# Mamba and expert block on one core: gate folded into the output weights, residual one sequence ahead, moments by aggregation, B two steps ahead, new slots

## The chip, the cores and the metric

The kernel runs on one core of a Trainium2 chip. A core has five engines with a queue of instructions each: TensorE (PE; its weight loads PEld), VectorE (DVE), ScalarE (ACT), GpSimd (POOL) and SyncE (SP), which here only issues DMAs. An engine works its own queue in order; between engines the order is kept by semaphores that an instruction raises and another waits for. Work goes on in SBUF (128 partitions) and PSUM (where TensorE writes). The metric is device microseconds for the whole program.

## The reference

For each of 16 sequences of 512 tokens with 128 features, all in f32:

```
h  = layernorm(x) * (1 + ca) + sa                        # sa, ca, ga, sb, cb, gb: rows per sequence
xn = layernorm(h) * norm_g + norm_b
for each direction d (forward, backward in time):
    u, z = split(xn @ Win.T);  u = silu(conv4(u) + convb)  # 256 channels
    dtr, B, C = split(u @ Wx.T);  dt = softplus(dtr @ Wdt.T + bdt)
    s_t = exp(dt_t * A) * s_(t-1) + (dt_t * u_t) * B_t     # 16 states per channel
    y_d = ((C_t . s_t) + u * D) * silu(z) @ Wout.T
x2  = x + ga * (h + y_f + y_b)
h2  = layernorm(x2) * (1 + cb) + sb
moe = shared swiglu(h2) + sum over the best 2 of 8 experts of weight * swiglu_e(h2)
out = x2 + gb * moe
```

## The kernel before

Everything is unrolled. `passes` calls `body(b, ...)` for b = 0 to 16. Pass b does the state scans of sequence b and, a sequence behind, the expert stage of sequence fb = b - 1; the preparation of sequence b + 1 (two normalizations, the forward direction's u, B, C, dt, z) runs in the same pass. A pass has 32 slots (`STEPS`): slot d*16 + n is the scan step of direction d and state n. Pass 0 has no expert stage, pass 16 has only that. Before pass 0 a prologue runs the preparation of sequence 0 alone.

Each engine's queue is written out by hand, slot by slot, from tables at the head (lines 30 to 38): `PREP_SLOT` and the `_AT` numbers say in which slot a step of a preparation stands, and `LN_SLOT`, `FX_SLOT`, `LN3_SLOT`, `H2T_SLOT`, `GATE_SLOT`, `UP_SLOTS`, `DOWN_SLOTS` do so for the rest. What stands in a slot per engine:

- GpSimd: `bmul` (L426) writes `bt` = v * B for the slot after (both halves, 128x1024), into one of two buffers; it waits until the scans of the slot two before the written one are done. Then `side`: `norms` (`moments`, eight small operations that turn the statistics into a reciprocal deviation and a shift; the scale and shift of h), `make_dt`, `make_v`. Then `ffn_side`: the residual `x2` (L511, L514), the moments of the third normalization, the router's weights, and `act` (L526), the product of the two up projections.
- VectorE: `scan` (L787), two halves in place in `psA`; `read_out` (L797), `g` = state * C, half 0; `expert_silu` (L882), `pf`; `read_out` half 1; then the side work: `statistics` (L803), `silu` (L823), the gate of y, `fx` (L907), the router (`gate`), `expert_sum` (L896) for each expert.
- ScalarE: `expert_turns` (L681 `tf`, L684 `gf`) from the up projections' banks; `exps` (L600), the decay exponentials of the next slot into `psA`, half by half, each after that half's read-out; `ln1p` (L648), whose `Ln` needs another function table than `Exp` and `Tanh`; the copy `h1K`; `normalize`; `silu`'s `Tanh` (L621) and the dt pieces. At slots 0 and 16 `keep_y` stands ahead of all.
- TensorE: `sum_y` (L987) of the slot before; `ffn_late` (projection L1085, turn of `zF` L1093, router L1098, half a down projection L1112 per slot); `prep` and the skip path; `expert_up` (L1068, L1071), one half of one expert per slot. There is one bank F0 and one F1, so each up projection waits for `pf` of the one before.
- SP: loads of B and C rows (`rows_in`) every other slot; at slot 0 the loads for the pass.

The gate `ga` multiplies `fx` = projection + h in `x2` = fx * ga + x, with x loaded a second time (`xR`). The functions that the change touches:

## Time and profile before

| what | value |
|---|---|
| timed runs | 2583.35, 2583.36, 2584.0 us (median 2583.36) |
| profiled execution, its own time | 2582.57 us |
| its span in the trace | 2580.8 us |
| granted TensorE clock, mean | 0.911 |
| HBM read, written | 285.91 MB, 6.34 MB |
| first scan starts, last scan ends | 87.0 us, 2495.0 us |

The span is the time between the first and the last instruction in the trace. Shares of busy time are averages over the prologue, 16 passes with scans and the tail. Times in a timeline are counted from the span's start; where a row merges several instructions its length is theirs together.

### The profile page before, as it was taken

How to read it: one execution, taken by the hardware profiler on the slowest of the kernel's cores; microseconds unless marked ns; L12 is line 12 of the kernel's file. 1: busy time of each engine (PE TensorE's matmuls, PEld its weight loads, DVE VectorE, ACT ScalarE, POOL GpSimd, SP SyncE). 2: the span in 40 equal slices, each digit the busy share in tenths (PEclk: the TensorE clock that was granted, in tenths of full speed). 3: DMA queues.
4: the chain of work that ended last, by engine and by line, in shares of the span. 5: the costliest groups of instructions: out<-in, count | busy, mean ns of one | idle time of the engine just before them, and what ended most of it. 6: DMA issues, size and time to landing. Idle time of an engine off the chain costs nothing. (4 is left out here: it accounts for less than half of the span.)

```text
span 2580.8 us, 31577 instructions
## 1 busy us (share of the span) xinstructions
PE 2100.5 (81%) x9893; PEld 1343.5 (52%) x9893; DVE 2284.9 (89%) x3603; ACT 1509.0 (58%) x2468; POOL 1957.8 (76%) x1437
## 2 busy tenths in 40 slices
PE   3677887978788897888879788897878879887868
PEld 1244554545555455555545555454555545555545
DVE  1699998999999899998989899899999989999973
ACT  2546656655566665656666555666556566555633
POOL 1577878778787877878877787877878787787854
PEclk8777998989899898998989899898989989899998
DMA  3334342333433333333333424333332433333310
GB/s 82 128 129 134 105 138 101 116 123 112 136 105 123 118 110 129 114 125 107 116 124 116 140 99 132 107 111 129 115 132 98 138 106 115 128 106 130 112 68 5
DMA packets 120557, 294.32 MB, mean 114 GB/s; under 512 B 18516, under 2 KB 53172, under 8 KB 120388
## 3 DMA queue, kind: packets, MB, share of 16 engines
q1 hardware_dynamic: 120388, 292.30, 33.7%
q8 instruction: 78, 1.28, 0.2%
q14 instruction: 91, 0.75, 0.1%
HBM read 285.91 MB, written 6.34 MB: 113 GB/s over the span
## 5 line engine op out<-in xcount | busy, mean ns | idle before, releaser
L426 POOL TENSOR_TENSOR bt<-v,bb 128x1024 f32<-128x1024 f32 x512 | 1208.4, 2363 | 158.7 <-DVE psA L787 154.6
L787 DVE TENSOR_TENSOR_SCAN psA<-psA,bt 128x512 f32<-128x512 f32 x1024 | 1197.3, 1215 | 100.7 <-POOL bt L426 81.1
L600 ACT ACTIVATE psA<-dt,aneg 128x512 f32<-128x512 f32 x1024 | 688.2, 688 | 813.0 <-DVE g L797 807.4
L987 PEld LDWEIGHTS psY<-ident,g 128*128 128x128 f32 x4096 | 515.4, 151 | 461.8 <-issue 241.6
L987 PE MATMUL psY<-ident,g 128*128 128x128 f32 x4096 | 605.5, 294 | 149.5 <-DVE g L797 149.4
L797 DVE TENSOR_TENSOR g<-psA,cb 128x512 f32<-128x512 f32 x1024 | 672.5, 676 | 0.0
L526 POOL TENSOR_TENSOR act<-pf,gf 128x512 f32<-128x512 f32 x288 | 366.8, 1273 | 248.4 <-DVE pf L882 216.2
L1068 PE MATMUL F<-h2T,w 128*128 128x512 f32 x576 | 333.9, 663 | 90.5 <-DVE pf L882 90.5
L1112 PE MATMUL F<-w,act 128*128 128x128 f32 x2304 | 319.8, 284 | 44.4 <-POOL act L526 41.1
L1112 PEld LDWEIGHTS F<-w,act 128*128 128x128 f32 x2304 | 292.2, 198 | 61.8 <-POOL act L526 55.3
L1071 PE MATMUL F<-h2T,w 128*128 128x512 f32 x576 | 307.5, 616 | 0.0
L882 DVE SCALAR_TENSOR_TENSOR pf<-tf,F 128x512 f32<-128x512 f32 x288 | 194.6, 676 | 64.4 <-ACT tf L681 62.7
L1003 PE MATMUL psP<-xnT,wcT 128*128 128x512 f32 x512 | 247.0, 606 | 5.2 <-DVE zs L823 2.2
L681 ACT ACTIVATE tf<-F 128x512 f32<-128x512 f32 x288 | 169.7, 589 | 63.7 <-PE F L1068 63.7
L684 ACT ACTIVATE gf<-F 128x512 f32<-128x512 f32 x288 | 172.4, 599 | 47.6 <-PE F L1071 47.5
L1068 PEld LDWEIGHTS F<-h2T,w 128*128 128x128 f32 x576 | 96.9, 200 | 197.4 <-DVE pf L882 139.0
L1071 PEld LDWEIGHTS F<-h2T,w 128*128 128x128 f32 x576 | 116.2, 202 | 150.9 <-issue 150.4
L1019 PE MATMUL psP<-xnT,wzT 128*128 128x512 f32 x128 | 99.2, 867 | 83.3 <-DVE zs L823 80.6
L896 DVE SCALAR_TENSOR_TENSOR facc<-F,wts,facc 128x128 f32<-128x128 f32 x512 | 143.0, 341 | 8.5 <-PE F L1112 8.5
L1003 PEld LDWEIGHTS psP<-xnT,wcT 128*128 128x128 f32 x512 | 89.6, 195 | 73.1 <-issue 64.8
L472 POOL TENSOR_TENSOR dt<-xb,ab 128x1024 f32<-128x1024 f32 x32 | 75.2, 2351 | 38.2 <-ACT ab L648 38.2
L1016 PE MATMUL psP<-xd,wdtT 8*128 8x512 f32 x128 | 91.2, 799 | 14.8 <-ACT xd L630 9.9
(133 smaller groups left out, 1709.1 us busy)
## 6 DMA issues: line engine op xcount, KB each, us to landing
bb<-bc_rows SPq DMA_DIRECT2D x256, 512.0 KB, 3.7
cb<-bc_rows SPq DMA_DIRECT2D x256, 512.0 KB, 3.6
x<-in_L_attn_x SPq DMA_DIRECT2D x16, 256.0 KB, 4.8
xR<-in_L_attn_x SPq DMA_DIRECT2D x16, 256.0 KB, 4.4
out_x<-osb SPq DMA_DIRECT2D x16, 256.0 KB, 4.8
w<-in_L_ffn_ew SPq DMA_DIRECT2D x2, 1024.0 KB
modA<-mod_table SPq DMA_DIRECT2D x16, 128.0 KB, 4.6
bc_rows<-xd SPq DMA_DIRECT2D x32, 64.0 KB, 3.2
```

The lines of the kernel that those rows point to most:

```text
L426: g.tensor_tensor(bt[:, n % 2, :, :], v[d][:, :, :], bb[:, n // 2 % 2, n % 2, :].unsqueeze(1).broadcast_to([P, NH, T]), ALU.mult).then_inc ...
L526: g.tensor_tensor(act[:, k // 2 % 3, k % 2, :], pf[:, k % 2, :], gf[:, k % 3, :], ALU.mult)\
L600: s.activation(psA[:, half * T:half * T + T], dt_[d][:, half, :], ACT.Exp, scale=aneg[d][:, half, n:n + 1]).then_inc(a_s, 1)
L684: s.activation(gf[:, k % 3, :], F1[:, :], ACT.Copy).then_inc(F1_free, 1)
L787: w.tensor_tensor_scan(ah, ah, bt[:, n % 2, half, :][:, order], 0.0, ALU.mult, ALU.add)\
L797: w.tensor_tensor(g_[:, n % 2, half, :], psA[:, half * T:half * T + T], cb[:, n // 2 % 2, n % 2, :], ALU.mult).then_inc(g_s, 1)
L882: w.scalar_tensor_tensor(pf[:, k % 2, :], tf[:, k % 2, :], 1.0, F0[:, :], ALU.add, ALU.mult).then_inc(pf_s, 1)
L987: last = m.matmul(psY[:, half * T + i * P:half * T + i * P + P], g_[:, n % 2, half, i * P:i * P + P], ident[:, :], is_transpose=True, star ...
L1003: last = m.matmul(psP[:, :], wcT[d][:, half, j, :], xnT[:, lo:lo + T], start=(j == 0), stop=(j == TAPS - 1))
L1068: m.matmul(F0[:, :], w1[:, x_, half * P:half * P + P], h2T[:, :], start=True, stop=True)\
L1071: m.matmul(F1[:, :], w2[:, x_, half * P:half * P + P], h2T[:, :], start=True, stop=True)\
L1112: last = m.matmul(F2[:, i * D:i * D + D], act[:, e % 3, half, i * P:i * P + P], w3[:, ORDER[e], half, :], start=(half == 0), stop=(half == 1))
```

## The change

- `ga` is multiplied into a copy of the output weights of both directions (`wg`), once per sequence on GpSimd at slot 25 (`gated_weights`), from a row `modG` that SP loads at slot 4. The projection uses `wg`.
- The residual hx = h * ga + x is made by GpSimd while sequence b + 1 is prepared (slots 21 and 23), and copied by ScalarE to `hxK`. `x2` is then one VectorE operation, projection + hxK. The second load of x and two GpSimd operations go; `load` of the next x waits for hx.
- `statistics` is followed by a memset and four aggregations (`bn_aggr`) on VectorE, after a wait for the statistics; `moments` has four operations instead of eight.
- `bmul` writes `bt` two slots ahead; it stands first in the slot, as before, and waits for the scan of its own slot.
- After `Ln` the table of `Exp` is loaded at once (`preload_act_table`). The Z pieces stand a slot later, `make_v` a slot earlier.
- The slots of the normalizations, of the third normalization, the router, the up and the down projections are new; the turn of `zF` moves from `ffn_late` to `expert_up`, behind the preparation in TensorE's queue.

The diff, cut to what is added and removed with the functions that it stands in:

```diff
-U_AT, XD_AT, DT_AT, LN1P_AT, Z_AT, V_AT = 0, 6, 7, 9, 9, 11
-LN_SLOT, XN_SLOT = 9, 16
+U_AT, XD_AT, DT_AT, LN1P_AT, Z_AT, V_AT = 0, 6, 7, 9, 10, 11
+STAT_SLOT, RSTD_SLOT, Z1_SLOT, H1_SLOT, STAT2_SLOT, RSTD2_SLOT, XNORM_SLOT, XN_SLOT = 8, 9, 10, 12, 13, 14, 15, 16
+HX_SLOT, WG_SLOT = 21, 25
-POSTB_SLOT, PROJ_SLOT, FX_SLOT, LN3_SLOT, H2T_SLOT, GATE_SLOT = 1, 3, 5, 6, 8, 9
-UP_SLOTS = [slot for slot in range(9, 28) if slot not in (22,)]
-DOWN_SLOTS = [slot for slot in range(12, 32) if slot not in (19, 21)]
+POSTB_SLOT, PROJ_SLOT, X2_SLOT, LN3_SLOT, H2T_SLOT, GATE_SLOT = 1, 3, 4, 4, 6, 7
+UP_SLOTS = [slot for slot in range(7, 28) if slot not in (9, 10, 22)]
+DOWN_SLOTS = [slot for slot in range(11, 32) if slot not in (13, 14, 25)]
...
             def load(b):
-                wait(sp, h1_s, 2 * b)
+                wait(sp, hx_s, 2 * b)
-                row = mod_dram[bass.ds(b, 1), 0:2 * D].broadcast_to([P, 2 * D])
+                row = mod_dram[bass.ds(b, 1), 0:3 * D].broadcast_to([P, 3 * D])
...
+                    if scan and slot == X2_SLOT:
+                        wait(sp, wg_s, b)
+                        row = mod_dram[bass.ds(b, 1), 2 * D:3 * D].broadcast_to([P, D])
+                        sp.dma_start(modG[:, :], row).then_inc(modG_in, 16)
...
-                    for k, kind in enumerate((2, 5)):
-                        row = mod_dram[bass.ds(fb, 1), kind * D:kind * D + D].broadcast_to([P, D])
-                        sp.dma_start(modF[:, k, :], row).then_inc(modF_in, 16)
+                    row = mod_dram[bass.ds(fb, 1), 5 * D:6 * D].broadcast_to([P, D])
+                    sp.dma_start(modF[:, :], row).then_inc(modF_in, 16)
-                    sp.dma_start(xR[:, :, :], t["x"][bass.ds(fb, 1)].rearrange("a (k p) d -> p (a k) d", p=P))\
-                        .then_inc(xR_in, 16)
...
-            def moments(st_, stat_, rstd_, sig, q):
-                g.tensor_tensor(stat_[:, :, 0:2], st_[:, :, 1:3], st_[:, :, 4:6], ALU.add).then_inc(sig, 1)
-                g.tensor_tensor(stat_[:, :, 2:3], st_[:, :, 1:2], st_[:, :, 4:5], ALU.subtract).then_inc(sig, 1)
+            def moments(stat_, rstd_, sig, q):
+                g.tensor_tensor(stat_[:, :, 2], stat_[:, :, 1], epsilon[:, :], ALU.add).then_inc(sig, 1)
+                g.tensor_tensor(stat_[:, :, 3], stat_[:, :, 0], negative[:, :], ALU.mult).then_inc(sig, 1)
-                g.tensor_tensor(stat_[:, :, 0:3], stat_[:, :, 0:3], scales[:, :, :], ALU.mult).then_inc(sig, 1)
+                g.tensor_tensor(rstd_[:, :], stat_[:, :, 2], mhalf[:, :], ALU.pow).then_inc(sig, 1)
-                g.tensor_tensor(stat_[:, :, 3:4], stat_[:, :, 2:3], stat_[:, :, 2:3], ALU.mult).then_inc(sig, 1)
-                pool.wait_ge(sig, q + 4)
-                g.tensor_tensor(stat_[:, :, 4:5], stat_[:, :, 1:2], stat_[:, :, 3:4], ALU.add).then_inc(sig, 1)
-                pool.wait_ge(sig, q + 5)
-                g.tensor_tensor(stat_[:, :, 5], stat_[:, :, 4], epsilon[:, :], ALU.add).then_inc(sig, 1)
-                pool.wait_ge(sig, q + 6)
-                g.tensor_tensor(rstd_[:, :], stat_[:, :, 5], mhalf[:, :], ALU.pow).then_inc(sig, 1)
-                pool.wait_ge(sig, q + 7)
-                g.tensor_tensor(stat_[:, :, 6], stat_[:, :, 0], rstd_[:, :], ALU.mult).then_inc(sig, 1)
+                g.tensor_tensor(stat_[:, :, 4], stat_[:, :, 3], rstd_[:, :], ALU.mult).then_inc(sig, 1)
             def norms(b, slot):
-                if slot == LN_SLOT + 1:
+                if slot == RSTD_SLOT:
-                    pool.wait_ge(lnA, 8 * b + 4)
+                    pool.wait_ge(lnA, 16 * b + 8)
-                    moments(st, stat, rstd, rstdA, 16 * b)
-                if slot == LN_SLOT + 3:
+                    moments(stat, rstd, rstdA, 8 * b)
+                if slot == H1_SLOT:
-                if slot == LN_SLOT + 5:
-                    pool.wait_ge(lnA, 8 * b + 8)
-                    moments(st, stat, rstd, rstdA, 16 * b + 8)
+                if slot == HX_SLOT:
+                    wait(pool, hxK_s, b)
+                    g.tensor_tensor(hx[:, :, :], z1[:, :, :], over_tiles(modA[:, 2, :]), ALU.mult).then_inc(hx_s, 1)
+                if slot == HX_SLOT + 2:
+                    pool.wait_ge(hx_s, 2 * b + 1)
+                    g.tensor_tensor(hx[:, :, :], hx[:, :, :], x[:, :, :], ALU.add).then_inc(hx_s, 1)
+                if slot == RSTD2_SLOT:
+                    pool.wait_ge(lnA, 16 * b + 16)
+                    moments(stat, rstd, rstdA, 8 * b + 4)
...
-                if slot == GATE_SLOT + 4:
+                if slot == GATE_SLOT + 6:
-                if slot == FX_SLOT:
-                    pool.wait_ge(F2_free, (DOWN + 1) * fb + PROJ + 1)
-                    pool.wait_ge(modF_in, 48 * fb + 48)
-                    wait(pool, o_s, 2 * fb)
-                    g.tensor_tensor(x2[:, :, :], fx[:, :, :], over_tiles(modF[:, 0, :]), ALU.mult).then_inc(x2_s, 1)
-                    pool.wait_ge(x2_s, 2 * fb + 1)
-                    pool.wait_ge(xR_in, 16 * fb + 16)
-                    g.tensor_tensor(x2[:, :, :], x2[:, :, :], xR[:, :, :], ALU.add).then_inc(x2_s, 1)
-                if slot == LN3_SLOT:
-                    pool.wait_ge(lnF, NT * fb + NT)
+                if slot == LN3_SLOT + 1:
+                    pool.wait_ge(lnF, 8 * fb + 8)
-                    moments(stF, statF, rstdF, rstdF_s, 8 * fb)
+                    moments(statF, rstdF, rstdF_s, 4 * fb)
...
+            def gated_weights(b):
+                pool.wait_ge(modG_in, 16 * b + 16)
+                wait(pool, F2_full, (DOWN + NE) * (b - 1) + PROJ + 1)
+                g.tensor_tensor(wg[:, :, :, :].rearrange("p a k d -> p (a k) d"),
+                                wout_both[:, :, :, :].rearrange("p a k d -> p (a k) d"),
+                                over_tiles(modG[:, :]), ALU.mult).then_inc(wg_s, 1)
             def side(b, slot, prep_b, prep_f, post_f):
+                if post_f and slot == WG_SLOT:
+                    gated_weights(b)
-                    if slot == PREP_SLOT[0] + V_AT:
+                    if slot == PREP_SLOT[0] + V_AT - 1:
-                if prep_b and slot == PREP_SLOT[1] + V_AT:
+                if prep_b and slot == PREP_SLOT[1] + V_AT - 1:
+            bmul(1, 0, 1)
                     if scan:
-                        nxt = slot + 1
+                        nxt = slot + 2
-                            bmul(STEPS * b + nxt, 0, 0)
+                            bmul(STEPS * b + nxt, 0, nxt - STEPS)
...
+                s.preload_act_table(ACT.Exp)
             def normalize(dst, x_, stat_, rstd_, sig):
-                                 bias=stat_[:, i, 6:7]).then_inc(sig, 1)
+                                 bias=stat_[:, i, 4:5]).then_inc(sig, 1)
             def norms(b, slot):
-                if slot == LN_SLOT + 2:
-                    act_e.wait_ge(rstdA, 16 * b + 8)
-                    wait(act_e, h1K_s, b)
+                if slot == Z1_SLOT:
+                    act_e.wait_ge(rstdA, 8 * b + 4)
+                    wait(act_e, hx_s, 2 * b)
-                if slot == LN_SLOT + 6:
-                    act_e.wait_ge(rstdA, 16 * b + 16)
+                if slot == XNORM_SLOT:
+                    act_e.wait_ge(rstdA, 8 * b + 8)
...
                     if scan:
-                        if slot == FX_SLOT + 2:
+                        if slot == X2_SLOT + 2:
-                            act_e.wait_ge(h1_s, 2 * b + 2)
-                            s.activation(h1K[:, :, :], z1[:, :, :], ACT.Copy).then_inc(h1K_s, 1)
+                            act_e.wait_ge(hx_s, 2 * b + 2)
+                            s.activation(hxK[:, :, :], hx[:, :, :], ACT.Copy).then_inc(hxK_s, 1)
...
-            def statistics(x_, st_, sig):
+            def statistics(x_, st_, stat_, sig, q):
+                dve.wait_ge(sig, q + NT)
+                w.memset(stat_[:, :, 4], 0.0)
+                for i in range(NT):
+                    w.bn_aggr(stat_[:, i, 0:2], st_[:, i, :]).then_inc(sig, 1)
             def norms(b, slot):
-                if slot == LN_SLOT:
+                if slot == STAT_SLOT:
-                    wait(dve, rstdA, 16 * b)
-                    statistics(x, st, lnA)
-                if slot == LN_SLOT + 4:
+                    wait(dve, rstdA, 8 * b)
+                    statistics(x, st, stat, lnA, 16 * b)
+                if slot == STAT2_SLOT:
-                    statistics(z1, st, lnA)
+                    statistics(z1, st, stat, lnA, 16 * b + 8)
...
             def ffn_side(fb, slot):
-                if slot == FX_SLOT:
+                if slot == X2_SLOT:
-                    dve.wait_ge(h1K_s, fb + 1)
+                    dve.wait_ge(hxK_s, fb + 1)
-                    w.tensor_tensor(fx[:, :, :], F2[:, :].rearrange("p (k c) -> p k c", c=D), h1K[:, :, :], ALU.add)\
+                    w.tensor_tensor(x2[:, :, :], F2[:, :].rearrange("p (k c) -> p k c", c=D), hxK[:, :, :], ALU.add)\
                 if slot == LN3_SLOT:
-                    dve.wait_ge(x2_s, 2 * fb + 2)
-                    wait(dve, rstdF_s, 8 * fb)
-                    statistics(x2, stF, lnF)
-                if slot == GATE_SLOT + 1:
+                    dve.wait_ge(F2_free, (DOWN + 1) * fb + PROJ + 1)
+                    wait(dve, rstdF_s, 4 * fb)
+                    statistics(x2, stF, statF, lnF, 8 * fb)
+                if slot == GATE_SLOT:
...
             def expert_up(fb, slot):
+                if slot == H2T_SLOT:
+                    pe.wait_ge(zF_s, NT * fb + NT)
+                    pe.wait_ge(F2_free, free + H2T)
+                    for i in range(NT):
+                        last = m.transpose(F2[:, i * P:i * P + P], zF[:, i, :], ident[:, :])
+                    last.then_inc(F2_full, 1)
...
+                        pe.wait_ge(wg_s, fb + 1)
-                                            woutT[k // NH][:, k % NH, :], start=(k == 0), stop=(k == 2 * NH - 1))
+                                            wg[:, k // NH, k % NH, :], start=(k == 0), stop=(k == 2 * NH - 1))
-                if slot == H2T_SLOT:
-                    pe.wait_ge(zF_s, NT * fb + NT)
-                    pe.wait_ge(F2_free, free + H2T)
-                    for i in range(NT):
-                        last = m.transpose(F2[:, i * P:i * P + P], zF[:, i, :], ident[:, :])
-                    last.then_inc(F2_full, 1)
```

## Rows read from the trace of the kernel before

**Rows 1.** Busy time of each engine, from the page.

```profile
PE 2100.5 (81%) x9893; PEld 1343.5 (52%) x9893; DVE 2284.9 (89%) x3603; ACT 1509.0 (58%) x2468; POOL 1957.8 (76%) x1437
```

**Rows 2.** Windows, all engines: start:end, length, busy (count), clock, DMA share, GB/s.

```profile
0.00:87.01 87.01, 34.75 (x73) 13.56 (x73) 11.63 (x47) 25.28 (x47) 15.49 (x35) 0.82 0.30 86
87.01:214.49 127.48, 86.81 (x330) 52.36 (x331) 119.62 (x147) 68.61 (x108) 92.43 (x55) 0.75 0.38 132
977.87:1130.53 152.66, 129.90 (x617) 83.12 (x616) 142.15 (x225) 93.58 (x154) 122.23 (x90) 0.91 0.36 119
```

**Rows 3.** Waits of VectorE in the pass at 977.87: total, times, longest.

```profile
DVE psA L787 <- POOL bt L426: 4.9, 5, 1.6
DVE pf L882 <- ACT tf L681: 1.9, 1, 1.9
DVE zs L823 <- ACT th L621: 1.6, 1, 1.6
DVE psA L787 <- ACT psA L600: 0.9, 4, 0.2
DVE acc L841 <- PE psP L1026: 0.5, 1, 0.5
DVE facc L896 <- PE F L1112: 0.4, 1, 0.4
```

**Rows 4.** Timeline, slot 4 and the start of ScalarE after it: start, length.

```profile
997.76 2.34 DVE L787 TENSOR_TENSOR_SCAN psA<-psA,bt 128x512 f32<-128x512 f32 x2 [0.23 <-ACT psA L600]
...
1000.02 1.27 DVE L797 TENSOR_TENSOR g<-psA,cb 128x512 f32<-128x512 f32 x2
...
1001.20 0.68 DVE L823 SCALAR_TENSOR_TENSOR u<-th,psP 128x512 f32<-128x512 f32 x1
...
1000.73 1.30 ACT L600 ACTIVATE psA<-dt,aneg 128x512 f32<-128x512 f32 x2 [0.78 <-DVE g L797]
```

**Rows 5.** VectorE: group MAX8; timeline of four, and of one set of statistics.

```profile
L853 DVE MAX8 top<-gl 128x8 f32<-128x8 f32 x64 | 5.8, 152 | 0.0
...
1027.62 0.36 DVE L853 MAX8 top<-gl 128x8 f32<-128x8 f32 x4
...
1005.83 0.86 DVE L803 BATCH_NORM_STATS2 stF<-x 128x6 f32<-128x128 f32 x4
```

**Rows 6.** Timeline of GpSimd, slots 5 to 7 of the same pass.

```profile
1002.56 1.27 POOL L511 TENSOR_TENSOR x<-fx,modF 128x512 f32<-128x512 f32 x1 [3.77 <-DVE fx L907]
...
1007.45 0.20 POOL L433 TENSOR_TENSOR statF<-stF 128x8 f32<-128x8 f32 x1
...
1010.13 0.20 POOL L447 TENSOR_TENSOR statF<-statF,rstdF 128x4 f32<-128x4 f32 x1
```

**Rows 7.** Groups of GpSimd, from the page: busy, mean ns, idle before.

```profile
L426 POOL TENSOR_TENSOR bt<-v,bb 128x1024 f32<-128x1024 f32 x512 | 1208.4, 2363 | 158.7 <-DVE psA L787 154.6
...
L526 POOL TENSOR_TENSOR act<-pf,gf 128x512 f32<-128x512 f32 x288 | 366.8, 1273 | 248.4 <-DVE pf L882 216.2
```

**Rows 8.** Timeline of ScalarE, slots 7 to 16 of the same pass.

```profile
1012.24 1.63 ACT L652 ACTIVATE zF<-x,statF,rstdF 128x128 f32<-128x128 f32 x4
...
1020.71 1.28 ACT L648 ACT_TABLE_LOAD   x1
...
1022.00 1.06 ACT L648 ACTIVATE ab<-ab 128x1024 f32<-128x1024 f32 x1
...
1055.80 1.08 ACT L608 ACTIVATE acc<-psY 128x512 f32<-128x512 f32 x2 [0.68 <-PE psY L987]
...
1056.77 0.60 ACT L681 ACTIVATE tf<-F 128x512 f32<-128x512 f32 x1
```

**Rows 9.** Timeline of ScalarE before the first scan.

```profile
76.63 0.60 ACT L621 ACTIVATE th<-psP 128x512 f32<-128x512 f32 x1 [1.65 <-PE psP L1019]
```

**Rows 10.** Timeline of VectorE and ScalarE in the tail.

```profile
2507.57 0.69 DVE L907 TENSOR_TENSOR fx<-F,h1K 128x512 f32<-128x512 f32 x1 [3.99 <-PE F L1085]
...
2514.85 1.65 ACT L652 ACTIVATE zF<-x,statF,rstdF 128x128 f32<-128x128 f32 x4 [16.87 <-POOL statF L447]
```

More of the change, by code:

```diff
@@ L98, in adaln_mamba_moe @@
         wdtT = [sb(f"wdtT{d}", [R, NH, P]) for d in range(2)]
-        woutT = [sb(f"woutT{d}", [P, NH, D]) for d in range(2)]
+        wout_both = sb("woutT", [P, 2, NH, D])
+        woutT = [wout_both[:, d, :, :] for d in range(2)]
         norm = sb("norm", [P, 2])
@@ L111, in adaln_mamba_moe @@
         gabs = sb("gabs", [NB, 2, D])
-        modA = sb("modA", [P, 2, D])
-        modF = sb("modF", [P, 2, D])
+        modA = sb("modA", [P, 3, D])
+        modF = sb("modF", [P, D])
+        modG = sb("modG", [P, D])
         modC = sb("modC", [D, 2])
@@ L117, in adaln_mamba_moe @@
         st = sb("st", [P, NT, 6])
[L118 removed]
+        stat = sb("stat", [P, NT, 5])
         mhalf = sb("mhalf", [P, NT])
@@ L126, in adaln_mamba_moe @@
         xnT = sb("xnT", [D, T + 2 * PAD])
-        h1K = sb("h1K", [P, NT, D])
-        xR = sb("xR", [P, NT, D])
+        hx = sb("hx", [P, NT, D])
+        hxK = sb("hxK", [P, NT, D])
+        wg = sb("wg", [P, 2, NH, D])
         diag = sb("diag", [P, 2, NH, P])
@@ L222, in adaln_mamba_moe @@
         h1_s = sem("h1_s")
-        h1K_s = sem("h1K_s")
+        hx_s = sem("hx_s")
+        hxK_s = sem("hxK_s")
+        wg_s = sem("wg_s")
         pP_full = sem("pP_full")
@@ L265, in adaln_mamba_moe @@
         MOD_STEPS = 12
-        CONSTS = 9
+        CONSTS = 7
         block = ctx.enter_context(nc.Block())
@@ L412, in _ @@
             g.memset(ones[:, :], 1.0).then_inc(const_ok, 1)
-            for k, scale in enumerate((-0.5, 1.0 / D, 0.5)):
-                g.memset(scales[:, :, k:k + 1], scale).then_inc(const_ok, 1)
+            g.memset(negative[:, :], -1.0).then_inc(const_ok, 1)
             def over_tiles(row):
@@ L692, in ffn_side @@
                     act_e.wait_ge(F2_full, (DOWN + NE) * fb + H2T + 1)
-                    act_e.wait_ge(modF_in, 48 * fb + 48)
+                    act_e.wait_ge(modF_in, 32 * fb + 32)
                     s.activation(h2T[:, :], F2[:, :], ACT.Identity, scale=modC[:, 1:2], bias=modC[:, 0:1])\
                         .then_inc(F2_free, 1)
-                if slot == GATE_SLOT + 2:
+                if slot == GATE_SLOT + 1:
                     act_e.wait_ge(gate_s, GATES * fb + GATE_D)
```

12 lines of the change are left out of this document (5 added, 7 removed).

## The prediction

> **What bounds the kernel now.** I read the busy shares first: VectorE is busy 2284.9 of 2580.8 us, ScalarE and GpSimd clearly less [rows 1]. The windows then cut the span into stretches: 87.0 us before the first scan, 127.5 us for pass 0 (no expert stage yet), fifteen passes of 152.66 us with it (one is shown, their starts lie at that distance), and the tail after the last scan [rows 2]. In one such pass VectorE works 142.15 us and is idle 10.5 us, so nothing an edit does elsewhere can give more than that 10.5 us, and each microsecond added to VectorE costs 15. The waits of VectorE inside that pass say where the 10.5 us are: 4.9 us for `bt` from GpSimd, 1.9 us for `tf`, 1.6 us for `th` (both ScalarE), 0.9 us for the decay exponentials, 0.9 us for TensorE [rows 3].
>
> Scan and read-out cost VectorE 3.43 us a slot: the shown slot starts at 997.76, its next operation at 1001.20. A slot with nothing beside them takes 3.75, since the next slot's exponential overwrites `psA` and starts only when half 0 is read out, 2.97 us into the slot (1000.73), two halves in 1.30 us; the shown scan itself, behind such a bare slot, waited 0.23 us [rows 4]. I write T6 for the start of slot 6's scan, and so on. The lesser costs that I add below come from the differences between neighbouring slots: 0.6 us for a `pf`, `u`, `zs` or gate operation, 1.05 us for an expert sum.
>
> **The change part by part.**
>
> *Moments by aggregation.* VectorE gains, three times per pass, one memset, a wait for its own statistics and four aggregations over 6 numbers each. The trace has no aggregation. Below it lie the MAX8s over 8 numbers, four in 0.36 us, 0.07 us apart; above it the statistics over 128 numbers, four in 0.86 us, 0.19 us apart [rows 5]. By these a set costs 0.36 or 0.86 us, with 0.1 to 0.15 us for memset and wait. I take the end near MAX8, since the inputs are as short: 0.5 us a set, 1.5 us a pass; the other end is 3.0 us a pass. The ends of the range keep both. It could not be below nothing, since nothing leaves VectorE.
> The four MAX8s have a mean of 0.152 us but stand 0.07 us apart [rows 5]. The Trainium skill ("VectorE: DVE Perf Modes", "The DRAIN you can't avoid") says that the next operation doesn't issue until the pipe is empty, though it also exempts operations that are not held; by the first sentence a set would be 0.61 us and not 0.36, 11 us over the run. The trace goes with the exemption.
>
> On GpSimd a moments set goes from eight operations, 2.9 us end to end, to four: the power of 1.0 us stays and four small ones at 0.29 us go, so 1.75 us are left [rows 6].
>
> *Residual a sequence ahead, gate in the weights.* The two GpSimd operations on `x2` (1.27 us each, entered after 3.77 us of waiting for VectorE [rows 6]) leave the path from projection to expert normalization and become two on `hx` at slots 21 and 23; the `wg` product at 25 adds one of the same size. GpSimd then does about 1.3 us more and 3.4 us less per pass. It was 122.2 of 152.7 us busy [rows 2], which hides this as long as `bt` is on time. SP issues one row `modG` and a wider `modA` in place of the `xR` load; its waits name work finished some slots before (`hx` at 23, `wg` at 25 against loads at slots 0 and 4), so I take nothing for SP. If that cover failed the loads of `bb` queued behind it would be late; the new waits would have to be a whole slot, 4 us, late for that.
>
> *B two steps ahead.* Before, `bt` of slot s+1 came after all side work of slot s-1; now that of s+2 starts at the end of scan s (2.35 us into it [rows 4]), takes 2.36 us [rows 7], and everything else of GpSimd's slot stands behind it. `bt` waits disappear (4.9 us) unless GpSimd is a whole slot behind. What pays is the rest of that queue: products, moments, `dt` and `v` come up to 2.4 us later. The places where it counts:
> - Slots 5 and 6: GpSimd starts the moments at T5+4.7 and ends at T5+6.4, which is T6+2.4. ScalarE stands in slot 5's normalization, 1.63 us [rows 8], until T6+4.0, and only then computes slot 7's exponential, whose input was free at T6+2.97. The scan starts at T6+4.75 in place of T6+3.43: 1.3 us.
> - Slots 9 and 10: `Ln` with its loads stands behind slot 10's exponential, whose half 1 ends at T9+4.84: a load of 1.28, `Ln` of 1.06 and a load back like the first [rows 8], to T9+8.5 = T10+4.5, then 0.7 us for slot 11's exponential. VectorE is ready at T10+3.6: 1.6 us. Before, the same row of work held `tf` (1.9 us) and at slots 28 and 29 `th` (1.6 us). At slot 29, with the Z piece a slot later, 0.75 us are left, since the expert sum there gives VectorE 1.05 us of work.
> - Slot 13: GpSimd has `dt` and `v` behind slot 12's `bt`, then the shift and scale for the second statistics; by my count these end 0.3 us after VectorE asks.
> - Slots 15 and 16: the second normalization starts behind slot 16's exponential (T15+4.84) and ends at T16+2.45; the copy of y and then `tf` follow, 0.97 and 0.60 us [rows 8]. `pf` wants `tf` at T16+2.83 and gets it at 4.05: 1.2 us. Before, slot 15 was 6.4 us long by its waits and hid it.
> - Bare slots 0, 3, 23: 0.3 us each; slot 27: 0.1 us as now.
> Together 6.2 us of waits a pass where 10.5 us were.
> The load at 1020.71 takes 1.28 us and `Ln` starts 0.01 us after it [rows 8]. The Trainium skill ("ScalarE: Activation LUTs", "What ACT_TABLE_LOAD costs") gives 1.28 us and a drain of 1.38 us more per switch. By it the two loads ahead of slot 11 would hold it 2.8 us longer, also before; the trace shows no such drain.
>
> *New slots, down projections two slots behind.* The number of products and of down halves per slot stays the same over a pass; but slots 18, 19, 20 and 23 now hold both, with the skip path or a convolution beside them. TensorE is busy 129.9 of 152.7 us [rows 2], 87% of a pass of 149.8 us, so it can fall behind by a piece and catch up in the slots without an up projection (22) or without a down half (25). I take nothing for it; a piece that came too late would show as `tf` late, as the 1.9 us of now. The down halves wait for products a full slot older, which removes the TensorE wait of 0.4 us.
>
> **The sum.** A pass: 142.1 + 1.5 + 6.2 = 149.8 us, 2.86 below 152.66; fifteen give 42.9 us. Pass 0 has no expert stage: two aggregation sets for a shorter ScalarE burst, +0.5 us. The prologue: `Ln` no longer stands behind a Z activation that waits 1.65 us for TensorE and takes 0.60 [rows 9], and one moments chain is 0.6 us shorter: -2.9 us. The tail: from the end of `fx` (2508.26) to `zF` (2514.85) are 6.6 us [rows 10]; now statistics, aggregation and short moments, 3.3 us: -3.3 us. Its expert loop is one of TensorE matmuls with equally many slots of each kind, unchanged. Total -48.6 us on the profiled execution's 2582.57 us: 2534 us. The median of the timed runs is 0.8 us above that execution; I say 2534.5 us.
>
> **The rivals.**
> 1. *ScalarE is not in the way* (0.12). The stalls at slots 6, 10 and 16 rest on sub-microsecond orders. If they stay out, about 2.5 us of waits are left, 146.1 us a pass: 98 + 6 us less, 2479 us. For it: ScalarE is busy only 94 of 152.7 us [rows 2]. Against: its work there comes in lumps in front of an exponential.
> 2. *Aggregations as dear as the statistics* (0.15): 3.0 us a pass in place of 1.5, or waits that I missed of that size: 151.3 us, so 2557 us. In the same direction to nothing gained (0.08): 2570 to 2585 us.
> 3. *GpSimd too late between slots 9 and 17* (0.10, slower). There GpSimd has nine `bt` of 2.36 us, `dt` and `v` (as large), two moments of 1.75, shift and scale (2.6), the router's weights (about 1) and seven products of 1.27 us [rows 6, 7]: 42 us, against 42.6 us of VectorE slots. `bt` may not start before the scan two slots older ends, so work that waits once is not caught up. For it: 0.65 us is all that I find spare before slot 13. It decides once new waits pass 9.0 us a pass, 2.8 us more than in my list; with 6 us more in these slots a pass is 155.8 us and the run 2624 us.
> 4. *The lookahead does nothing*, if `bt` waits are mere heirs of others: only the stretch of normalizations gains; this is inside the 2570 to 2585 case.
>
> **How the numbers follow.** My forecast has 0.55, 2534.5 us, own range 2515 to 2555. The range that should hold the time 8 times in 10 leaves out most of rival 1 and rival 3: 2502 to 2572. A measurement of this kernel tells 0.2%, 5 us. Faster: 0.55 + 0.12 + 0.15 and some of the small case, 0.85; same 0.05; slower 0.10.
>
> **What would show it.** Right: passes of 149 to 151 us; no `bt` wait over 0.5 us; waits for the exponential after `zF` and after the second load of about 1.3 and 1.6 us; `tf` about 1.2 us late at slot 16; four aggregations in 0.3 to 0.5 us; `zF` 3.3 us after `x2` in the tail. Wrong: `bt` waits left at slots 13 to 17, aggregations 0.2 us apart, or passes above 152.7 us.

## The result and the profile after

The changed kernel takes 2593.55 us (median of six, 2592.39 to 2597.27), the kernel before 2583.43 us (2583.26 to 2584.0) on the same chip: ratio 1.004, interval [1.0027, 1.0053]. It is slower by 0.4%; 2534.5 us were predicted. The profiled execution took 2597.27 us, 3.7 us more than that median.

The page's busy times, then the windows of prologue, pass 0 and one expert pass (they answer to [rows 1] and [rows 2]; columns as there):

```profile
PE 2107.3 (81%) x9893; PEld 1319.4 (51%) x9893; DVE 2299.5 (89%) x3843; ACT 1507.5 (58%) x2468; POOL 1936.7 (75%) x1259
```

```profile
0.00:88.02 88.02, 36.59 (x71) 14.45 (x72) 12.38 (x57) 25.17 (x47) 16.63 (x27) 0.88 0.30 86
88.02:216.42 128.40, 88.20 (x329) 51.50 (x328) 120.02 (x156) 68.65 (x108) 94.36 (x50) 0.74 0.38 132
983.38:1136.96 153.58, 128.91 (x617) 81.44 (x616) 143.01 (x239) 93.55 (x154) 120.94 (x78) 0.92 0.34 116
```

VectorE's work in a pass is 143.0 us, 0.6 below the 143.6 us that I had counted. Its idle time is 10.6 us, as before, where I had 6.2. So the miss of a pass is 3.8 us: I had 4.4 us of waits too few and 0.6 us of work too much. VectorE's waits in that pass (they answer to [rows 3]: total, times, longest), then the places where they stand (start, length, in brackets the wait before it):

```profile
DVE pf L892 <- ACT tf L687: 3.7, 2, 2.1
DVE psA L793 <- ACT psA L605: 3.6, 6, 1.7
DVE facc L906 <- PE F L1123: 1.4, 1, 1.4
DVE psA L793 <- POOL bt L430: 1.3, 1, 1.3
```

```profile
1013.70 2.35 DVE L793 TENSOR_TENSOR_SCAN psA<-psA,bt 128x512 f32<-128x512 f32 x2 [1.29 <-POOL bt L430]
...
1033.52 2.35 DVE L793 TENSOR_TENSOR_SCAN psA<-psA,bt 128x512 f32<-128x512 f32 x2 [1.69 <-ACT psA L605]
...
1042.14 0.69 DVE L892 SCALAR_TENSOR_TENSOR pf<-tf,F 128x512 f32<-128x512 f32 x1 [1.66 <-ACT tf L687]
...
1044.50 2.35 DVE L793 TENSOR_TENSOR_SCAN psA<-psA,bt 128x512 f32<-128x512 f32 x2 [0.48 <-ACT psA L605]
...
1062.95 0.69 DVE L892 SCALAR_TENSOR_TENSOR pf<-tf,F 128x512 f32<-128x512 f32 x1 [2.06 <-ACT tf L687]
...
1126.33 2.35 DVE L793 TENSOR_TENSOR_SCAN psA<-psA,bt 128x512 f32<-128x512 f32 x2 [0.73 <-ACT psA L605]
...
1135.92 1.13 DVE L906 SCALAR_TENSOR_TENSOR facc<-F,wts,facc 128x128 f32<-128x128 f32 x4 [1.45 <-PE F L1123]
```

Slots 6, 12, 16 and 31 begin at 1008.89, 1037.56, 1057.97 and 1130.36. The first line is slot 6's wait, predicted 1.3 us; the profile puts it down to a `bt`, but this scan's `bt` was ready at 1009.64 and what came late is the exponential behind `zF` (1012.92, first half done at 1013.6). The next (slot 10, predicted 1.6) and the sixth (slot 29, predicted 0.75) are as forecast. The three that are not: 2.14 us in slot 12, where I had none, 2.06 in slot 16, where I had 1.2, and 1.45 in slot 31, where I had none. All three begin on TensorE. I call a group of its matmuls that belong together a piece. Its timeline in slot 12, with `tf` on ScalarE behind it:

```profile
1037.69 2.07 PE L1029 MATMUL psP<-xnT,wzT 128*128 128x512 f32 x2 [4.34 <-DVE zs L833]
...
1039.56 1.91 PE L1084 MATMUL F<-h2T,w 128*128 128x512 f32 x2
...
1041.27 1.92 PE L1087 MATMUL F<-h2T,w 128*128 128x512 f32 x2
...
1041.51 0.60 ACT L687 ACTIVATE tf<-F 128x512 f32<-128x512 f32 x1 [1.11 <-PE F L1084]
```

TensorE stood 4.34 us. The Z piece of slot 11 waits for `zs` of that slot, and the up projection that slot 12's `pf` needs (L1084, L1087) is queued behind it. Then each piece takes 1.9 to 2.1 us, where it takes 1.02 to 1.13 elsewhere. The windows of the idle stretch, the stretch behind it, the next one, and the like stretch of slot 31 (the column ahead of the last two is the granted clock):

```profile
1033.35:1037.69 4.34, 0.01 (x1) 0.00 (x0) 4.17 (x6) 3.94 (x9) 4.26 (x3) 0.88 0.00 0
1037.69:1043.19 5.50, 5.50 (x8) 2.29 (x8) 3.84 (x5) 1.29 (x3) 5.50 (x3) 0.50 0.41 127
1043.19:1048.70 5.51, 5.18 (x30) 3.70 (x30) 5.03 (x8) 4.27 (x8) 5.43 (x5) 0.97 0.18 64
...
1130.50:1135.72 5.22, 5.22 (x19) 4.08 (x20) 3.97 (x5) 1.99 (x4) 4.74 (x3) 0.51 0.10 41
```

Behind each idle stretch the granted clock is 0.50 and 0.51, the level of 1.2 GHz, for 5.2 to 5.5 us of dense work; then it is back near 2.4 GHz. In slot 31 the Z piece (2.07 us, after 3.63 us idle), `sum_y` (1.91) and the down half (1.81) run so, and the expert sum waits 1.45 us. The Trainium skill ("TensorE: Matmul & The Clock Gate", "Part 1: The HAM clock gate") has the same two levels, the lower one behind idleness; the trace agrees.

### The profile page after: what moved, and what is told of

It reads as the page before. It is cut to its first block and busy times, and to the rows that moved or that the text cites. A ratio compares the mean times of both kernels' runs of the same rounds, so it can differ in the third digit from the quotient of the medians.

```text
span 2595.4 us, 31606 instructions
## 1 busy us (share of the span) xinstructions
PE 2107.3 (81%) x9893; PEld 1319.4 (51%) x9893; DVE 2299.5 (89%) x3843; ACT 1507.5 (58%) x2468; POOL 1936.7 (75%) x1259
## 3 DMA queue, kind: packets, MB, share of 16 engines
q8 instruction: 78, 1.28, 0.2%
## 5 line engine op out<-in xcount | busy, mean ns | idle before, releaser
L997 PEld LDWEIGHTS psY<-ident,g 128*128 128x128 f32 x4096 | 505.7, 150 | 451.7 <-issue 251.5
L997 PE MATMUL psY<-ident,g 128*128 128x128 f32 x4096 | 594.1, 288 | 143.4 <-DVE g L803 142.3
L1084 PE MATMUL F<-h2T,w 128*128 128x512 f32 x576 | 342.5, 680 | 104.4 <-DVE pf L892 104.4
L1087 PE MATMUL F<-h2T,w 128*128 128x512 f32 x576 | 333.8, 664 | 0.0
L1084 PEld LDWEIGHTS F<-h2T,w 128*128 128x128 f32 x576 | 95.5, 197 | 216.2 <-DVE pf L892 162.3
L1087 PEld LDWEIGHTS F<-h2T,w 128*128 128x128 f32 x576 | 122.4, 213 | 158.5 <-issue 158.0
L626 ACT ACTIVATE th<-psP 128x512 f32<-128x512 f32 x128 | 75.8, 592 | 66.6 <-PE psP L1029 64.5
```

Source lines behind the costliest of these rows:

```text
L997: last = m.matmul(psY[:, half * T + i * P:half * T + i * P + P], g_[:, n % 2, half, i * P:i * P + P], ident[:, :], is_transpose=True, star ...
L1084: m.matmul(F0[:, :], w1[:, x_, half * P:half * P + P], h2T[:, :], start=True, stop=True)\
L1087: m.matmul(F1[:, :], w2[:, x_, half * P:half * P + P], h2T[:, :], start=True, stop=True)\
```

## The experiments

Mean slot lengths over passes 2 to 14, in us, for the slots that the text uses (5, 7, 9, 14, 18 and 22 to 25 differ too). The diffs below are cut to the lines that decide; counters, and the place that a line was moved from, are left out.

```
slot   before  after  e1    e2    e3    e4    f1    f2    f3    f4    g1    g2    g3    g4
 1      4.04   4.04  4.04  4.04  4.03  4.27  4.04  4.04  4.37  4.28  4.04  4.27  4.25  4.04
 4      3.76   5.36  4.94  5.36  5.36  5.36  5.36  4.95  4.94  4.94  5.36  5.36  5.36  3.75
 6      5.12   4.81  5.95  3.75  4.81  4.81  3.75  3.75  3.75  3.75  3.75  3.75  3.75  4.21
 8      3.75   5.23  4.83  5.23  5.23  5.23  5.23  4.81  4.81  4.81  5.23  5.23  5.23  4.95
10      8.53   5.31  5.26  5.31  5.31  5.31  5.31  5.28  5.28  4.91  5.31  5.31  3.89  8.53
11      4.63   4.03  4.03  4.03  4.03  4.03  4.03  4.24  4.25  4.62  4.04  4.03  4.03  4.62
12      4.20   6.94  6.73  6.22  4.62  4.89  4.94  4.65  4.64  4.64  5.12  4.64  5.30  4.11
13      6.14   5.23  4.82  5.23  5.37  5.30  5.23  6.12  6.13  6.13  5.22  5.38  6.09  5.87
15      6.40   4.30  4.40  4.03  4.03  4.03  4.98  6.38  6.39  6.39  4.26  4.03  4.03  7.59
16      4.04   7.15  6.97  6.37  6.28  6.28  6.13  5.07  5.07  5.07  6.71  5.13  5.13  4.36
17      5.68   4.65  4.65  4.65  4.65  4.65  4.65  4.65  4.91  5.04  4.65  4.65  4.65  7.14
29      6.76   5.28  5.28  5.28  5.28  5.28  5.28  5.28  5.28  4.46  5.29  5.29  4.46  6.76
31      4.47   6.56  6.51  6.25  6.52  5.06  6.59  5.78  5.06  5.06  6.52  5.06  5.06  4.47
pass  152.66 153.58 153.6 150.4 150.2 149.4 150.2 150.2 150.2 149.4 150.2 146.8 145.9 153.6
```

### First four: one part at a time

Before on this chip: 2583.94 us.

**e1, the moments of before in the changed kernel.**

```diff
-                for i in range(NT):
-                    w.bn_aggr(stat_[:, i, 0:2], st_[:, i, :]).then_inc(sig, 1)
+                # GpSimd: eight small operations per set, as before
```

> The changed kernel with the moments of before (eight GpSimd operations, no aggregation on VectorE). Theory: aggregation costs VectorE 0.5 us a set, on the bound engine, 1.3 to 1.5 us a pass, and gives back 1.1 us of GpSimd per set only where a chain waits for it: without it slot 6 waits about 0.7 us more and the pass is 0.5 to 1 us shorter: 2576 to 2586 us. Rival: the shorter chains are worth more than the aggregations cost: 2600 us or more.

2598.59 us, 1.0057 [1.004, 1.0074]. Slots 4 and 8 become 0.42 and 0.40 us shorter, slot 13 as much, which is the price of a set on VectorE; slot 6 becomes 1.14 us longer, since the longer moments make `zF` later, and slots 7 and 9 together 0.5. The exchange is even in the pass: neither my theory nor its rival (2600 us or more) came, though the rival's balance lay nearer. Aggregations are not where the time went.

**e2, B one step ahead again, and v a slot later.**

```diff
-                        nxt = slot + 2
+                        nxt = slot + 1
-                    if slot == PREP_SLOT[0] + V_AT - 1:
+                    if slot == PREP_SLOT[0] + V_AT:
```

> The changed kernel with B one step ahead and v a slot later again, as before. Theory: the lookahead itself is worth 2 to 4 us a pass, since bt waits of about 4 us come back while the waits at slots 6 and 16 fall by about 2: 2610 to 2640 us. Rival (the lookahead is what made the change slower, by queueing products and moments behind bt): 2570 to 2585 us.

2551.85 us, 0.9877 [0.9861, 0.9894]. My theory fell, and the run is faster than its rival said too: without the second step no `bt` wait came back, so it is not the lookahead that keeps them away in the changed kernel, and slot 6 became 1.06 us shorter. Slots 12, 15, 16 and 31 fell too, by 0.27 to 0.8 us, though nothing in them was touched but GpSimd's order.

**e3, slot 11's up projection ahead of the Z piece.**

```diff
+                    if ffn and slot == 11:
+                        expert_up(b - 1, slot)
                     if scan_:
                         side(b, slot, True, None if last else b + 1, True)
-                    if ffn:
+                    if ffn and slot != 11:
                         expert_up(b - 1, slot)
```

> The changed kernel with the up projection of slot 11 ahead of the Z piece in TensorE's queue. Theory: the 2.2 us of VectorE wait at slot 12 come from the Z matmul, which waits for zs of slot 11, standing in front of the up projection: the wait goes, 2 us a pass, 30 us in all: 2562 us. Rival (the up projection is late for its clock alone, or the wait only moves to the next slot): within 8 us of the changed kernel.

2548.53 us, 0.9862 [0.9845, 0.9878], 14 us better than expected. TensorE in slot 12 (which begins at 1021.59):

```profile
1021.72 1.13 PE L1029 MATMUL psP<-xnT,wzT 128*128 128x512 f32 x2 [2.62 <-DVE zs L833]
...
1025.15 1.13 PE L1084 MATMUL F<-h2T,w 128*128 128x512 f32 x2 [0.54 <-DVE pf L892]
```

The up projection fills part of the gap (2.62 us in place of 4.34) and is done when `pf` asks. Slot 12 falls by 2.3 us to what it costs without a wait, 15 by 0.3 and 16 by 0.9. The edit changed two things at slot 12, though: the order, and with it the level of the piece behind the gap, which is the upper one here.

**e4, idle matmuls, no order changed.** Four in slot 11, two in slot 14, four in slot 30, into a bank that the next up projection overwrites.

```diff
+                        if slot in FILL_SLOTS and scan_:
+                            wait(pe, F1_free, ups)
+                            for _ in range(FILL_SLOTS[slot]):
+                                m.matmul(F1[:, :], w1[:, 0, 0:P], h2T[:, :], start=True, stop=True)
```

> The changed kernel with idle matmuls (128x512, four at slot 11, two at slot 14, four at slot 30, into F1, whose content is written over) ahead of the side work, so that TensorE does not stand idle for 2 to 4 us there. Theory: TensorE falls to its lower clock in these gaps and the pieces behind take double, which makes 4 of the 5 us of waits at slots 12, 16 and 31: passes of 149 to 150 us, 2530 to 2545 us. Rival (the order of the queue alone): no faster than the changed kernel, or slower by the filling.

2534.78 us, 0.9809 [0.9793, 0.9826]. TensorE ahead of and in slot 12, in two passes (L1146 is the idle work). In the first, slot 12 begins at 864.63:

```profile
860.26 3.60 PE L1146 MATMUL F<-h2T,w 128*128 128x512 f32 x8
864.76 1.13 PE L1030 MATMUL psP<-xnT,wzT 128*128 128x512 f32 x2 [0.90 <-DVE zs L834]
865.73 1.02 PE L1085 MATMUL F<-h2T,w 128*128 128x512 f32 x2
```

The Z piece starts 0.13 us into the slot, as it does without the edit, and the up projection still stands behind it. But both run at the upper level, and slot 12 takes 4.62 us, without a wait, in place of 6.94. So it is in ten of the passes 1 to 14. In the other four slot 12 takes 5.2 to 5.6 us; one of them begins at 1013.36:

```profile
1008.78 1.91 PE L1124 MATMUL F<-w,act 128*128 128x128 f32 x8
1010.49 4.24 PE L1146 MATMUL F<-h2T,w 128*128 128x512 f32 x8
1014.56 1.02 PE L1030 MATMUL psP<-xnT,wzT 128*128 128x512 f32 x2
1015.42 1.02 PE L1085 MATMUL F<-h2T,w 128*128 128x512 f32 x2
```

```profile
1009.00:1014.50 5.50, 5.50 (x16) 3.30 (x16) 5.17 (x7) 4.20 (x9) 5.42 (x3) 0.75 0.11 25
1014.50:1020.00 5.50, 5.50 (x26) 3.43 (x25) 4.68 (x7) 3.59 (x7) 5.50 (x4) 1.00 0.48 157
```

Here TensorE had come to the lower level before the idle work (1.91 us for a down half, granted clock 0.75 in the first window), the Z piece starts 1.2 us late behind it, and `pf` waits 0.82 us. The mean of slot 12 is 4.89 us. The level alone is worth as much at this slot as order and level together in e3: either edit takes the wait away, so the two gains don't add. Slot 31 falls from 6.56 to 5.06 us; nothing there but idle work was added. TensorE did more, and the kernel ran 59 us faster, within the range that I had given.

### Second four: towards the best of both

Before on this chip: 2584.63 us. I added to e2 what had gained singly.

```diff
 f1: e2 and e3
 f2: f1 and e1
 f3: f2, idle matmuls in slot 30, and on ScalarE
-                    if slot == N and scan:
-                        keep_y(b, 0)
                     if ffn:
                         expert_turns(b - 1, up_at(slot - 1))
+                    if slot == N and scan:
+                        keep_y(b, 0)
 f4: f3, Z1_SLOT 10 -> 11, and around Ln
+                s.preload_act_table_set("natural_log_exp_and_others")
                 s.activation(ab[:, :, :], ab[:, :, :], ACT.Ln, bias=1.0).then_inc(sp_s, 1)
-                s.preload_act_table(ACT.Exp)
```

**f1.** 

> The changed kernel with B one step ahead (and v a slot later) and the up projection of slot 11 ahead of the Z piece. Theory: the two are separate: the lookahead costs 1.06 us at slot 6, where it holds the moments and so zF in front of an exponential, and the Z piece 2.3 us at slot 12; a pass is 150.2 - 1.1 = 149.1 us, the run 2530 to 2536 us. Rival: both runs freed the same wait (TensorE's clock at slots 12 to 16), so together they give no more than the up order alone: 2546 to 2552 us.

2543.21 us, 0.9837 [0.9821, 0.9854], between theory and rival. Slot 6 is as in e2 and slot 12 0.3 us longer than in e3, but the scan behind slot 15 now waits 1.1 us for `bt`.

**f2.** 

> The kernel of f1_look1_up with the moments of before. Theory: with B one step ahead the longer GpSimd chain no longer stands in front of an exponential, so dropping the aggregations gives what they cost VectorE, 1.2 us a pass: 2512 to 2520 us. Rival: the longer chain still holds zF: no gain.

2550.99 us, 0.9873 [0.9856, 0.9889]. The sets' 1.25 us on VectorE go, and `bt` waits of 3.9 us a pass come, at the ends of slots 13 to 15: the pass is the same, 150.2 us. The run is 8 us slower than f1, which the full passes of the profiled executions do not show.

**f3.** 

> The kernel of f2_plus_noaggr with four idle matmuls at slot 30 and with the copy of y at slot 16 behind tf and gf in ScalarE's queue. Theory: slot 31 loses its 1.4 us of wait, slot 16 about 0.9 of its 1.2 us: 2.3 us a pass, 2478 to 2488 us. Rival: slot 16's copy only moves the wait to slot 17, where the next sum needs it: 2490 to 2500 us.

2542.89 us, 0.9839 [0.9823, 0.9856]. Slot 31 gives 0.7 us, but slots 1 and 17 take 0.6 back, in some passes only; slot 16 had nothing left to give, since slot 15 already waited for GpSimd. The pass is 0.1 us shorter than in f2. Of the 6.2 us between the profiled executions of f2 and f3, 1.4 lie in the prologue and 2.1 in the tail.

**f4.** 

> The kernel of f3_plus_fill_keep with Ln taken from the function table that holds Exp too (loaded before Ln; Tanh's table is loaded again only at the next Tanh), and the first normalization a slot later. Theory: one load of 1.28 us no longer stands in front of an exponential at slots 9 and 28: 1.5 us and 0.7 us of wait go, 30 us in all: 2450 to 2458 us. Rival: the load moves in front of the Tanh and holds the following exponential there: no more than 10 us.

2529.11 us, 0.9784 [0.9767, 0.98]. One table load in place of two in front of the exponential: slot 29 gives 0.8 us, slot 10 only 0.4, and slot 11 takes that back: the scans behind them now wait 1.3 and 0.5 us for `bt` (pass at 810.71). The last three expectations lay 31 to 79 us too low. They added up gains; in f2 and at slot 10 of f4 waits for `bt` took them back.

### Third four: two steps ahead, with the queue behind it put right

Before on this chip: 2583.52 us. They separate "GpSimd is full there whatever the order" from "only what stands behind `bt` was late".

```diff
 g1: e3, and the third moments ahead of the B product in slot 5
                 for slot in range(STEPS):
+                    if ffn and slot == LN3_SLOT + 1:
+                        pool.wait_ge(lnF, 8 * (b - 1) + 8)
+                        wait(pool, zF_s, NT * (b - 1))
+                        moments(statF, rstdF, rstdF_s, 4 * (b - 1))
                     if scan:
                         nxt = slot + 2
 g2: g1, idle matmuls (two in slot 14, four in slot 30), keep_y behind tf and gf
 g3: g2, the table set and Z1_SLOT of f4
 g4: the kernel BEFORE, with nxt = slot + 2 and v a slot earlier, nothing else
```

**g1.** 

> The changed kernel (two ahead, aggregations) with slot 11's up projection ahead of the Z piece, and with GpSimd's moments of the third normalization ahead of its B product in slot 5. Theory: the cost of the second step of lookahead is the moments that stand behind the B product at slot 5 and nothing else; with them in front slot 6 is 3.75 us as with one step (4.81 with two), and no bt wait comes in its place at slots 13 to 15, since B stays two ahead: pass 149.2, run 2531 to 2535 us. Rival (GpSimd is full from slot 10 to 16 whatever the order): the 1.06 us come back at slots 13 to 16 as waits for bt, v or the second moments, as they did with one step ahead: pass 150.2, run 2543 to 2549 us.

2543.89 us, 0.9843 [0.9829, 0.9856]. Slot 6 is 3.75 us as the theory said, and no `bt` wait came. The pass is the rival's nonetheless, for another reason. TensorE in slot 12:

```profile
1016.78 2.07 PE L1029 MATMUL psP<-xnT,wzT 128*128 128x512 f32 x2 [2.62 <-DVE zs L833]
```

The same piece after the same 2.62 us as in e3, and here at the lower level (1.13 there). Slot 12 is 0.5 us longer than in e3 on the mean and slot 16 0.43 longer. So the order alone, at the lower level, is worth 1.8 of the 2.3 us that e3 got from slot 12. Its passes vary between 149.5 and 150.7 us. The tail had it too: 93.2 us, of which `wg` matmuls 5.4 us in place of 3.8.

**g2.** 

> The same, and idle matmuls of TensorE (two in slot 14, four in slot 30, their result is overwritten) and the copy of y at slot 16 behind tf and gf. Theory (TensorE's granted clock after its idle stretches, and a copy in front of tf, are what is left at slots 31 and 16): slot 31 goes from 6.5 to 5.06 us, slot 16 from 6.3 to 5.3: pass 146.8, run 2490 to 2505 us. Rival (GpSimd full from slot 10 to 16): slot 31 gains as said, but what slot 16 gives returns at slots 13 to 15: pass 147.7 to 148.3, run 2508 to 2520 us.

2496.82 us, 0.9663 [0.965, 0.9676]; pass 146.82 us where 146.8 were expected. VectorE's waits in one pass, at 947.47:

```profile
DVE psA L794 <- ACT psA L606: 3.4, 6, 1.7
DVE acc L852 <- PE F L1037: 0.3, 1, 0.3
```

No `tf`, no `facc`, no `bt` is left, so GpSimd is not the bound here (120.9 of 147.0 us busy). Slot 16 had come to 6.28 us by idle matmuls alone (e4) and is 5.13 here: the copy's new place is worth the other 1.15.

**g3, the best.** 

> The same, and Ln taken from the table set that holds Exp too, so that one load instead of two stands around it, and the first normalization a slot later. Theory: slot 29 -0.8 us (measured before), slot 10 -0.9 to -1.5 us (the second load and the normalization in front of the exponentials gone): pass 144.7 to 145.3, run 2460 to 2475 us. Rival (GpSimd full from slot 10 to 16): slot 10's gain returns as a bt wait there or behind, only slot 29 gains: 12 us less than the second kernel of this set.

2483.92 us, 0.9605 [0.9592, 0.9618]. Slot 29 gives 0.83, slot 10 1.42 us, but slots 12 and 13 take 1.37 back. Waits of VectorE in the pass at 945.06, then GpSimd from slot 10 on:

```profile
DVE psA L794 <- ACT psA L606: 1.2, 5, 0.3
DVE st L810 <- POOL z L459: 0.8, 1, 0.8
DVE psA L794 <- POOL bt L431: 0.6, 1, 0.6
```

```profile
992.63 2.36 POOL L431 TENSOR_TENSOR bt<-v,bb 128x1024 f32<-128x1024 f32 x1
994.94 2.36 POOL L475 TENSOR_TENSOR dt<-xb,ab 128x1024 f32<-128x1024 f32 x1
997.38 2.36 POOL L480 TENSOR_TENSOR v<-u,dt 128x1024 f32<-128x1024 f32 x1
999.70 4.67 POOL L431 TENSOR_TENSOR bt<-v,bb 128x1024 f32<-128x1024 f32 x2
1004.34 1.26 POOL L457 TENSOR_TENSOR xn<-z,modA 128x512 f32<-128x512 f32 x1
```

It works there without a gap. That is the rival's result, 12.9 us for the two edits, of which the slots 12 and 13 show where the other 20 went.

**g4.** 

> The kernel before, with B two steps ahead and v a slot earlier, nothing else. By the prediction's own accounts: the 4.9 us of bt waits a pass go; the third normalization's moments (2.9 us with eight operations) come up to 2.4 us later behind the B product and cost 1 to 2.4 us at slots 7 and 8; the two products on x2 in slots 5 and 6 also stand behind it, 1 us more; left -1 to -2.5 us a pass: 2545 to 2568 us. Rival (GpSimd is so full at slots 9 to 17 that lookahead only renames the waits): bt waits turn into waits for tf, zs and statistics, within 0.3 us a pass: 2578 to 2590 us.

2599.33 us, 1.0061 [1.0048, 1.0075]: the lookahead alone, on the kernel before, makes it slower, by more than either range allowed. No `bt` wait is left in the pass at 986.58, but slot 8 is 1.2 us longer, with a wait of 1.4 us for the exponential behind the late `zF`, as the expectation said. GpSimd and TensorE in slot 15 (from 1055.25), with the same down half a pass later:

```profile
1051.60 2.35 POOL L426 TENSOR_TENSOR bt<-v,bb 128x1024 f32<-128x1024 f32 x1
...
1054.91 1.26 POOL L526 TENSOR_TENSOR act<-pf,gf 128x512 f32<-128x512 f32 x1
```

```profile
1056.22 2.07 PE L1113 MATMUL F<-w,act 128*128 128x128 f32 x8 [3.44 <-POOL act L526]
1058.09 1.91 PE L1069 MATMUL F<-h2T,w 128*128 128x512 f32 x2
...
1210.00 1.16 PE L1113 MATMUL F<-w,act 128*128 128x128 f32 x8 [3.44 <-POOL act L526]
```

The product `act` stands behind `bt`; the down half one slot behind needs it, is ahead of the up projection in TensorE's queue, and holds it 3.44 us. In the pass shown, what follows runs at the lower level, `tf` is late, and slot 15 takes 9.4 us; a pass later the same gap of 3.44 us is followed by the upper level, and it takes 6.7. On the mean slots 15 and 17 grow by 1.2 and 1.5 us. In the changed kernel the down halves are two slots behind and this wait does not stand in a full pass.

## Why the prediction was wrong

**The step that failed is "TensorE: I take nothing for it".** I had reckoned its share, 87% of a pass, and looked for pieces too many for a slot. Two things were missing.

1. *Order.* Slots 9 and 10 have no up projection now, and in slot 11 it stands behind a Z piece that can't start before `zs`. The piece that `tf` needs is then late: 1.66 us for `pf` and 0.48 for the exponential behind `gf`. e3 moves nothing but this and gets 2.3 us of slot 12 back; 1.8 of them come at the lower level too (g1).
2. *Clock.* The gaps ahead of slots 12 and 31 and in slot 14 (4.34, 3.63 and 2.34 us) were followed by pieces at the lower level, nearly twice as long. Such pieces are no novelty of the change: the trace of before has a Z piece of 2.05 us at 1020.41, an up projection of 1.97 us at 1047.73, and a Z piece of 2.08 us behind 3.94 us of idleness at 1121.14. Two of them, from the trace of before:

```profile
1047.73 1.97 PE L1068 MATMUL F<-h2T,w 128*128 128x512 f32 x2 [0.17 <-DVE pf L882]
...
1121.14 2.08 PE L1019 MATMUL psP<-xnT,wzT 128*128 128x512 f32 x2 [3.94 <-DVE zs L823]
```

   I had read TensorE's sum and no single piece. New is that they stand where `pf` and the expert sum wait for them. e4 fills the gaps with work of no use and the same pieces run at 1.00 (at slot 12 in ten passes of fourteen); slots 12, 15, 16 and 31 fall by 2.05, 0.27, 0.87 and 1.50 us, 4.7 us of a pass, of which slots 1, 7, 9 and 13 take 0.5 back.

The two don't add at slot 12: the wait there needs both, and either edit removes it. At slot 31 e4 changes no order and takes away all of the 1.45 us.

Of the 3.8 us a pass that I missed, slot 12 is 2.14, slot 31 1.45 and slot 16 0.86, less the 0.6 us of work that I had counted too much; the small waits cancel. Over the passes (the first and the last miss a little less) it is 54.6 us of the 63.3 us by which the profiled execution misses its forecast; prologue, pass 0 and tail are 3.9, 0.4 and 4.2.

**Point by point, else.**
- *Aggregations*: 0.5 us a set predicted, 0.4 measured. The group of VectorE (busy, mean ns, idle before):

```profile
L813 DVE BATCH_NORM_AGGREGATE stat<-st 128x2 f32<-128x6 f32 x128 | 12.0, 156 | 1.5
```

  Right, at the end near MAX8 [rows 5]: three stand 0.06 us apart, and the four take 0.38 us with the memset between them (from 1023.94). By the sentence on the emptying pipe in the Trainium skill ("VectorE: DVE Perf Modes", "The DRAIN you can't avoid") they would take 0.62; the trace goes with the exemption that the Trainium skill names there, again.
- *Waits at slots 6, 10, 29*: 1.3, 1.6, 0.75 predicted, 1.29, 1.69, 0.73 measured. *Bare slots*: 0.23 each for 0.3. *`bt` waits gone*: they are, but e2 shows that they stay away without the lookahead too, so the reason that I gave was not the one. Slots 13 and 27: no wait for 0.3 and 0.1.
- *Slot 16*: the mechanism was right (the second normalization, the copy of y, then `tf`), its size not: 2.06 for 1.2 us, the rest being an up projection of 1.67 + 1.92 us at the lower level in slot 15, which made `sum_y` and the copy late (the copy waited 1.20 us). In e3 and e4, where that piece is not slow, the wait is 1.12.
- *Lookahead*: its 4.9 us came on paper only; undoing it (e2) made the kernel 42 us faster. What paid for it was in my list at slot 6; what I missed is that GpSimd's later `act` also moves TensorE's gaps (e2 in slots 12 to 31, g4 in 15 and 17).
- *Prologue*: -2.9 predicted, +1.0 measured. The order did what I said, `Ln`'s load follows its input at once: the first convolution starts 0.7 us earlier, and from the first Z piece to the first scan it is 10.7 in place of 12.5 us, 2.5 of the 2.9 us together. But the stretch between took 3.5 us more, above all two groups of convolutions, 6.73 and 5.40 us where they took 5.17 and 3.70 before:

```profile
50.90 6.73 PE L1013 MATMUL psP<-xnT,wcT 128*128 128x512 f32 x8 [0.87 <-ACT xnT L675]
...
59.73 5.40 PE L1013 MATMUL psP<-xnT,wcT 128*128 128x512 f32 x8 [2.10 <-DVE u L833]
```

  In f1, with the same prologue but for one product, they took 5.37 and 3.70, and its first scan starts at 83.8 us, 3.2 before that of the kernel before; in g1, with the changed kernel's prologue, they took 5.18 and 3.70, and it starts at 84.5. So the term was nearly right, and the profiled execution drew slower convolutions. Over the second group the granted clock is 0.68 (1.00 before); over the first it reads 1.00, so there the clock is not shown to be the cause.
- *Tail*: -3.3 predicted, +0.9 measured. From the end of `x2` to `zF` it is 3.17 us, 3.3 predicted. TensorE gave it back, 1.4 us ahead of `x2` and 3.0 behind `zF`:

```profile
2511.69 2.08 PE L1034 MATMUL F<-u,diag 128*128 128x512 f32 x2 [1.18 <-ACT acc L613]
...
2539.41 1.16 PE L1123 MATMUL F<-w,act 128*128 128x128 f32 x8 [2.08 <-POOL act L520]
```

  The skip path ran at the lower level (2.08 for 1.12 us, 1.57 for 1.05). And the tail's expert loop is not "unchanged": its first down half now stands ahead of the third up projection, after two instead of three, and waits 2.08 us for `act`. That is the same mistake, a count of pieces in place of their order.
- *Rival 3* (GpSimd full between slots 9 and 17) did not decide here. It is the bound behind the others: it shows in f1, f2, f4 and g3. *Rivals 1 and 2* did not occur. *Rival 4* (the lookahead does nothing) was nearer than my forecast, though not in its time: without the lookahead no `bt` wait comes back (e2), and alone it only puts other, longer waits in their place (g4).

What stays open: why one and the same gap is followed by either level (2.62 us in e3 and g1, 3.44 us in two passes of g4); the lengths of prologue (83.8 to 88.0 us) and tail (85.5 to 93.2) over these kernels are not explained beyond the granted clock in their pieces. The down halves one slot behind were not tried in the changed kernel.
